# Reloading the weights of a post-norm transformer layer from bf16 copies in DRAM, issued by SyncE

## The reference

```
q = x @ Wq + bq + pe;  k, v = split(x @ Wkv + bkv);  k = k + pe      # 8 heads of 128, one k and v
x = layernorm(x + concat(softmax(causal(q k^T / sqrt(128))) v) @ Wo)
logits = x @ Wc + bc + tie                                            # 128 expert sets, groups of 32 tokens
perm = (logits == max over the 32 tokens of the group)
inner = relu((perm^T x) @ W1 + b1)                                    # per expert set, 1024 -> 32
x = layernorm(x + perm (inner @ W2 + b2))                             # 32 -> 1024, scattered back
```

## Time and profile before

| | |
|---|---|
| median of 3 runs | 5055.51 us (5039.67 to 5063.03) |
| profiled execution, its own time | 5059.08 us |
| its span on the slowest core (core 5) | 5057.5 us |
| spans of the 8 cores | 5020.6 to 5057.5 us |
| mean granted TensorE clock | 0.66 of full speed on every core |

### The profile page before, as it was taken

One profiled execution on the slowest core, in us unless ns is written; L12 is line 12 of the kernel. 1 busy time (PEld: TensorE's weight loads), 2 busy tenths in 40 slices (PEclk: granted clock), 3 DMA queues, 4 the chain that ended last, 5 costly groups with the idle time before them and its releaser, 6 DMA issues.

```text
span 5057.5 us, 64599 instructions; the slowest of 8 cores (5020.6 to 5057.5 us)
## 1 busy us (share of the span) xinstructions
PE 2631.1 (52%) x19792; PEld 1416.4 (28%) x19792; DVE 1497.9 (30%) x3689; ACT 1836.4 (36%) x3808; POOL 54.9 (1%) x104
## 2 busy tenths in 40 slices
PE   4666636332666654542386665463328666546240
PEld 2333314211333322421133332241103333225110
DVE  2322134322322113431332211452223221245132
ACT  0455533210345562321234555241122455523113
POOL 0000000000000000000000000000000000000000
PEclk9678856555777885655577887565557678656555
DMA  4100032465400002157520001216661000200754
GB/s 82 42 17 17 9 50 35 84 124 111 128 17 17 17 9 51 35 105 146 104 92 17 17 17 29 45 20 128 122 133 63 17 18 17 58 18 18 154 100 129
DMA packets 171730, 305.44 MB, mean 60 GB/s; under 512 B 5394, under 2 KB 136722, under 8 KB 166546
## 3 DMA queue, kind: packets, MB, share of 16 engines
q1 hardware_dynamic: 153874, 203.77, 17.3%
q0 software_dynamic: 17536, 97.54, 10.8%
HBM read 298.15 MB, written 100.66 MB: 79 GB/s over the span
## 4 chain that ended last, share of the span: by engine, by line
PE 43%; ACT 17%; DMA 16%; DVE 11%; issue 11%; SPq 1%; ACTq 0%; DVEq 0%; POOL 0%; POOLq 0%
DMA rp_scratch<-rpn 11%; PE pp_pv L368 8%; ACT pT L344 7%; PE pp_s L336 6%; PE pp_w L443 5%; PE pp_s L282 5%; DMA rpe<-rp_scratch 5%; PE pp_s L599 4%; PE pp_s L648 3%; PE pp_s L568 2%; ACT x2b L557 2%; ACT pTn L390 2%; DVE pT L352 2%; PE pp_w L694 2%; PE pp_w L701 2%
## 5 line engine op out<-in xcount | busy, mean ns | idle before, releaser
L344 ACT ACTIVATE pT<-pp_s,c_negC 128x512 bf16<-128x512 f32 x1280 | 846.1, 691 | 354.5 <-PE pp_pv L368 216.9
L368 PE MATMUL pp_pv<-vS,pT 128*128 128x129 bf16 x5120 | 618.6, 257 | 399.0 <-DVE pT L352 230.3
L368 PEld LDWEIGHTS pp_pv<-vS,pT 128*128 128x128 bf16 x5120 | 393.5, 112 | 795.4 <-issue 789.5
L336 PE MATMUL pp_s<-qT,kT 128*128 128x512 bf16 x1280 | 595.3, 483 | 0.1
L352 DVE TENSOR_TENSOR pT<-pT,c_zl 128x512 bf16<-128x512 bf16 x512 | 217.6, 425 | 960.5 <-ACT pT L344 960.3
L648 PE MATMUL pp_s<-w_2t,inr 32*64 32x256 bf16 x1024 | 139.1, 401 | 670.2 <-DVE rpn L661 586.2
L661 ACT CAST rpn<-pp_s 128x256 bf16<-128x256 f32 x256 | 95.4, 373 | 799.0 <-DMA rpe<-rp_scratch 710.4
L282 PE MATMUL pp_s<-xT,w_q 128*128 128x512 bf16 x1024 | 258.2, 422 | 186.8 <-DMA w_kv<-wkv 161.4
L443 PE MATMUL pp_w<-w_o,atT 128*128 128x512 bf16 x1024 | 273.0, 427 | 94.1 <-DVE x L451 80.1
L661 DVE CAST rpn<-pp_s 128x256 bf16<-128x256 f32 x256 | 108.7, 424 | 699.2 <-DMA rpe<-rp_scratch 616.9
L648 PEld LDWEIGHTS pp_s<-w_2t,inr 32*64 32x64 bf16 x1024 | 70.9, 122 | 737.9 <-issue 737.7
(11 more groups left out here) (87 smaller groups left out, 2984.7 us busy)
## 6 DMA issues: line engine op xcount, KB each, us to landing
rp_scratch<-rpn SPq DMA_DIRECT2D x32, 2048.0 KB, 16.0
rpe<-rp_scratch SPq DMA_DIRECT2D x32, 2048.0 KB, 14.4
xtile<-x SPq DMA_DIRECT2D x64, 512.0 KB, 3.8
w<-w POOLq DMA_DIRECT2D x16, 2048.0 KB, 15.4
w_2t<-w2t POOLq DMA_DIRECT2D x64, 512.0 KB, 13.9
y<-x SPq DMA_DIRECT2D x64, 512.0 KB, 4.4
xT<-xT POOLq DMA_DIRECT2D x4, 4096.0 KB, 27.8
w_o<-wo POOLq DMA_DIRECT2D x4, 2048.0 KB, 15.9
```

What stands on the lines that cost most here:

```text
L336: return inc("tensor", "sPE", 1, lambda e, kc=kc, ping=ping, h=h, qb=qb: e.matmul(pp_s[ping][:, :], kT[:, kc * 128: kc * 128 + 128], qT[:, ...
L344: ev = inc("scalar", "sACT", 1, lambda e, ping=ping: e.activation(out=pT[ping][:, :], in_=pp_s[ping][:, :], func=AF.Exp, bias=c_negC, scal ...
L368: ping=ping, sub=sub, kc=kc, kcmax=kcmax: e.matmul(bank[:, colo: colo + 129], pT[ping][:, sub * 128: sub * 128 + 128], vS[:, kc * 132: kc ...
```

## The change

In sequence 0 the weights are loaded by GpSimd as before. When each has landed, SyncE stores the bf16 tile to an internal DRAM tensor (`cwkv`, `cwo`, `ctie`, `cw1`, `cw2`). In sequences 1 to 3 the weights are loaded from these copies by SyncE, without a conversion. `xT` and the weights that stay in SBUF are loaded as before. The waits of each load move from GpSimd's list to SyncE's. Further waits keep reuse of the places in order: in sequence 0 GpSimd waits for the copy of a `w_1` or `w_2t` tile before it loads the next over it, and VectorE and ScalarE wait for the copies before they write over the same places.

```
--- before.py
+++ after.py
+    cw1 = nc.dram_tensor("cw1", [4, 128, 2 * 128 * 32], BF16, kind="Internal").ap()
+    cw2 = nc.dram_tensor("cw2", [4, 128, 32 * 256], BF16, kind="Internal").ap()
+    cwo = nc.dram_tensor("cwo", [128, CH * 1024], BF16, kind="Internal").ap()
+    cwkv = nc.dram_tensor("cwkv", [128, CH * 256], BF16, kind="Internal").ap()
+    ctie = nc.dram_tensor("ctie", [1, T], BF16, kind="Internal").ap()
...
-        mk_wkv = inc("gpsimd", "sGW", 16, lambda e: e.dma_start(out=w_kv, in_=dwkv))
-
+        if s == 0:
+            mk_wkv = inc("gpsimd", "sGW", 16, lambda e: e.dma_start(out=w_kv, in_=dwkv))
+            wait("sync", mk_wkv)
+            st_wkv = inc("sync", "sS3", 16, lambda e: e.dma_start(out=cwkv, in_=w_kv))
+        else:
+            wait("sync", st_all_ws)
+            wait("sync", st_wkv)
+            mk_wkv = inc("sync", "sWE", 16, lambda e: e.dma_start(out=w_kv, in_=cwkv))
+
+        if s == 1:
+            wait("vector", st_s2_all); wait("scalar", st_s2_all)
         wait("tensor", mk_wkv)
+        if s > 0:
+            wait("tensor", mk_xT)
...
         p1_done = now("sPE")
-        wait("gpsimd", p1_done)
-        mk_wo = inc("gpsimd", "sGW", 16, lambda e: e.dma_start(out=w_o, in_=dwo))
-        mk_tie = inc("gpsimd", "sGW", 16, lambda e: e.dma_start(out=c_tie, in_=dtie))
+        if s == 0:
+            wait("gpsimd", p1_done)
+            mk_wo = inc("gpsimd", "sGW", 16, lambda e: e.dma_start(out=w_o, in_=dwo))
+            mk_tie0 = inc("gpsimd", "sGW", 16, lambda e: e.dma_start(out=c_tie, in_=dtie))
+            wait("sync", mk_tie0)
+            inc("sync", "sWS", 16, lambda e: e.dma_start(out=cwo, in_=w_o))
+            st_tie = inc("sync", "sWS", 16, lambda e: e.dma_start(out=ctie, in_=c_tie))
+            mk_tie = mk_tie0
+        else:
+            wait("sync", p1_done)
+            mk_wo = inc("sync", "sWE", 16, lambda e: e.dma_start(out=w_o, in_=cwo))
+            mk_tie = inc("sync", "sWE", 16, lambda e: e.dma_start(out=c_tie, in_=ctie))
...
+                    if s == 0:
+                        wait("sync", st_wkv)
...
-        gw1 = {0: inc("gpsimd", W1S[0], 16, lambda e: e.dma_start(out=w_1[0], in_=dw1[0]))}
+        def w1_load(q4):
+            if s == 0:
+                if q4 >= 2:
+                    wait("gpsimd", w1_store[q4 - 2])
+                m = inc("gpsimd", w1sems[0][q4 % 2], 16,
+                        lambda e, q=q4: e.dma_start(out=w_1[q % 2], in_=dw1[q]))
+                wait("sync", m)
+                w1_store[q4] = inc("sync", ["sS1a", "sS1b"][q4 % 2], 16,
+                                   lambda e, q=q4: e.dma_start(out=cw1[q], in_=w_1[q % 2]))
+                return m
+            return inc("sync", w1sems[1][q4 % 2], 16,
+                       lambda e, q=q4: e.dma_start(out=w_1[q % 2], in_=cw1[q]))
...
+        if s > 0:
+            wait("sync", ln1)
+        gw1 = {0: w1_load(0)}
         def w2t_load(q4, part):
             c0 = 0 if part == 0 else 2048
+            if s == 0:
+                sem = "sW20" if part == 0 else "sW21"
...
+                wait("sync", m)
+                inc("sync", "sS2", 16, lambda e, q4=q4, c0=c0: e.dma_start(
+                    out=cw2[q4][:, c0: c0 + 2048], in_=w_2t[0][:, c0: c0 + 2048]))
+                w2t_store[q4] = inc("sync", "sS2", 16, lambda e, q4=q4, c0=c0: e.dma_start(
+                    out=cw2[q4][:, 4096 + c0: 4096 + c0 + 2048],
+                    in_=w_2t[0][:, 4096 + c0: 4096 + c0 + 2048]))
+                return m
+            sem = "sWC" if part == 0 else "sWD"
+            inc("sync", sem, 16, lambda e, q4=q4, c0=c0: e.dma_start(
+                out=w_2t[0][:, c0: c0 + 2048], in_=cw2[q4][:, c0: c0 + 2048]))
+            return inc("sync", sem, 16, lambda e, q4=q4, c0=c0: e.dma_start(
                 out=w_2t[0][:, 4096 + c0: 4096 + c0 + 2048],
-                in_=dw2[q4][:, 4096 + c0: 4096 + c0 + 2048]))
+                in_=cw2[q4][:, 4096 + c0: 4096 + c0 + 2048]))
...
             if q4 + 1 < 4:
                 if q4 >= 1:
-                    wait("gpsimd", now("sPE"))
+                    wait("gpsimd" if s == 0 else "sync", now("sPE"))
+                gw1[q4 + 1] = w1_load(q4 + 1)
...
             if q4 + 1 < 4:
-                wait("gpsimd", now("sPE"))
+                eng_w = "gpsimd" if s == 0 else "sync"
+                wait(eng_w, now("sPE"))
+                if s == 0:
+                    wait("gpsimd", w2t_store[q4])
                 gw2[q4 + 1] = w2t_load(q4 + 1, 0)
                 gw2b[q4 + 1] = w2t_load(q4 + 1, 1)
```

More of the change, by code:

```diff
@@ L137, in build_nc @@
     semnames = ["sPE", "sACT", "sDVE", "sLD", "sST", "sRS", "sGW",
-                "sXT0", "sXT1", "sW10", "sW11", "sW20", "sW21"]
+                "sXT0", "sXT1", "sW10", "sW11", "sW20", "sW21",
+                "sWA", "sWB", "sWC", "sWD", "sWE", "sWS", "sS1a", "sS1b", "sS2", "sS3"]
     sems, cms = {}, []
@@ L204, in build_nc @@
     prev_stores = None
+    st_all_ws = None
+    st_wkv = None
+    st_s2_all = None; st_s1a = None; st_s1b = None
     def emit_ln_stats_finish():
@@ L470, in build_nc @@
         wait("gpsimd", ln1)
-        gw1 = {0: inc("gpsimd", W1S[0], 16, lambda e: e.dma_start(out=w_1[0], in_=dw1[0]))}
+        w1sems = [["sW10", "sW11"], ["sWA", "sWB"]]
+        w1_store = {}
+        def w1_load(q4):
[10 more added lines that the diff above has]
+                       lambda e, q=q4: e.dma_start(out=w_1[q % 2], in_=cw1[q]))
@@ L472, in w2t_load @@
+        if s == 1:
+            wait("sync", st_all_ws)
+            wait("sync", st_s2_all)
+            wait("sync", st_s1a); wait("sync", st_s1b)
+        if s > 0:
+            wait("sync", ln1)
+        gw1 = {0: w1_load(0)}
         def w2t_load(q4, part):
             c0 = 0 if part == 0 else 2048
-            sem = "sW20" if part == 0 else "sW21"
-            inc("gpsimd", sem, 16, lambda e, q4=q4, c0=c0: e.dma_start(
-                out=w_2t[0][:, c0: c0 + 2048], in_=dw2[q4][:, c0: c0 + 2048]))
@@ L477, in w2t_load @@
-            return inc("gpsimd", sem, 16, lambda e, q4=q4, c0=c0: e.dma_start(
+            if s == 0:
+                sem = "sW20" if part == 0 else "sW21"
+                inc("gpsimd", sem, 16, lambda e, q4=q4, c0=c0: e.dma_start(
+                    out=w_2t[0][:, c0: c0 + 2048], in_=dw2[q4][:, c0: c0 + 2048]))
+                m = inc("gpsimd", sem, 16, lambda e, q4=q4, c0=c0: e.dma_start(
+                    out=w_2t[0][:, 4096 + c0: 4096 + c0 + 2048],
+                    in_=dw2[q4][:, 4096 + c0: 4096 + c0 + 2048]))
+                wait("sync", m)
[5 more added lines that the diff above has]
+                return m
@@ L478, in w2t_load @@
+            sem = "sWC" if part == 0 else "sWD"
+            inc("sync", sem, 16, lambda e, q4=q4, c0=c0: e.dma_start(
+                out=w_2t[0][:, c0: c0 + 2048], in_=cw2[q4][:, c0: c0 + 2048]))
+            return inc("sync", sem, 16, lambda e, q4=q4, c0=c0: e.dma_start(
                 out=w_2t[0][:, 4096 + c0: 4096 + c0 + 2048],
[L479 removed]
+                in_=cw2[q4][:, 4096 + c0: 4096 + c0 + 2048]))
+        w2t_store = {}
         gw2 = {0: w2t_load(0, 0)}
@@ L483, in build_nc @@
         wait("tensor", mk_tie)
+        if s == 0:
+            wait("vector", st_tie)
+            wait("scalar", st_wkv)
         for tb in range(NQB):
@@ L546, in build_nc @@
                 if q4 >= 1:
-                    wait("gpsimd", now("sPE"))
-                gw1[q4 + 1] = inc("gpsimd", W1S[(q4 + 1) % 2], 16,
-                                  lambda e, q=q4 + 1: e.dma_start(out=w_1[q % 2], in_=dw1[q]))
+                    wait("gpsimd" if s == 0 else "sync", now("sPE"))
+                gw1[q4 + 1] = w1_load(q4 + 1)
             if q4 == 0:
@@ L555, in build_nc @@
                     wait("scalar", pv2)
+                    if s == 0:
+                        wait("vector", st_tie); wait("scalar", st_tie)
                 gwait("scalar", ("x2b", tt % 2))
@@ L635, in emit_e2 @@
                 wait("tensor", relu_done)
+                if s == 0:
+                    for eng_ in ("vector", "scalar"):
+                        wait(eng_, w1_store[2]); wait(eng_, w1_store[3])
             rsq_marks = []
@@ L732, in build_nc @@
                 st_m[:, tt: tt + 1], x2[:, tt * 1024: tt * 1024 + 1024], AX.X, ALU.add))
+        if s == 0:
+            wait("scalar", w2t_store[3])
         _ = emit_ln2_finish()
@@ L744, in build_nc @@
         prev_stores = st_marks[-1]
+        if s == 0:
+            st_all_ws = now("sWS")
+            st_s2_all = now("sS2")
+            st_s1a = now("sS1a"); st_s1b = now("sS1b")
         gset("R2xT", sc_last)
```

## The result

The changed kernel takes 5151.78 us (median of 8 runs, 5144.5 to 5170.35) against 5056.82 us (median of 8): a ratio of 1.0195, 95% interval 1.0177 to 1.0213. It is slower by 95 us; the forecast was 5153 us.

A forecast was written before the change was run, and what follows sets the result against it. The kernel was taken as bound by waits, no engine busy over 52%. Terms +88.4 - 6.3 + 15.4 = +97.5 on the profiled 5059.1 gave 5156.6, less 3.6 to the median: 5153 us, range 5110 to 5190.

The forecast's parts named there:

- The seam: Between sequences: w_kv's load waits behind the 16 stores of y, delaying projections by +29.7, +29.9 and +28.8 us, +88.4 in all.
- the drain: Between sequences: w_kv waits some 5 us for store traffic on SyncE's queue; on a second queue the sum would be about 76.
- The clock rival: Delayed projections of sequences 2 and 3 run at a higher TensorE clock, giving 5132 us; chance 0.12.
- The restack of sequences 1 to 3: Second expert layer: first restack behind four faster w_2t loads on SyncE's queue, -2.1 us each, -6.3 in all.
- Sequence 0: Second expert layer, where copies are made: restacks wait for w_2t loads to land, +7.4 and twice +4.0, +15.4 us.
- Restack begins at +18.4: Sequence 0's second expert layer: restack starts 18.4 us after the quarter, following w_2t's landing, second-half copy and issue.
- The covered loads: w_o, w_1 and the first w_2t are issued long before use, so changing their loads costs or gives nothing.
- The slow queue: Second expert layer: slow loads ahead of first restacks and copies fully ahead in sequence 0, giving 5204 us; chance 0.09.
- no stall: Between sequences: w_kv's load passes the stores, so no change, 5065 us; chance 0.04.
- the clock in attention: Longer idle time between sequences lifts the clock in three attention stages, ending faster, 5026 us at 0.95; chance 0.03.

The follow-up runs named there:

- the load moved back: Changed kernel with the w_kv load for the next sequence issued by SyncE ahead of the 16 stores of y: 5065.02 us, ratio 1.0040.
- the part alone: Kernel before with only w_kv copied in sequence 0 and reloaded by SyncE behind the stores of y: 5132.38 us, ratio 1.0169.
- half the stores: Changed kernel with the w_kv load placed behind 8 of the 16 stores of y: ratio 1.0154.
- the changed kernel with two waits: Changed kernel with SyncE's 64 waits ahead of each restack's first store replaced by the last two: 5102.95 us, ratio 1.0122.
- the kernel before with two waits: Kernel before with only the 64 waits ahead of each restack's first store replaced by the last two: 5012.28 us, ratio 0.9923.
- the best kernel: Changed kernel with w_kv ahead of stores, w_2t copies behind the restack, two waits for 64, half the next w_2t early: 4999.4 us, ratio 0.9889.

## Why the prediction was right

- **The seam** (+88.4 forecast, +84.1 measured). Mechanism, place and size hold. It is shown from three sides: the load moved back takes the cost away, the part alone gives it, and half the stores give part of it. The 4 us too many are small only because the pace stands on both sides. I carried sequences 2 and 3 of the profiled core on at 0.27 us a matmul (68.0 and 69.4 us), and in the profile after all three took 57.4 to 57.6 us for 256, or 0.22; but the stages that I subtracted were that core's own, 9 and 11 us longer than the median core's, and the two nearly cancel. The landing was 0.7 to 0.8 us later than forecast in each seam (70.5, 70.2 and 69.4 us after `xT`'s issue, against 69.7, 69.5 and 68.6). The reason given for the drain, that the load shares SyncE's queue, is not borne out: on GpSimd's queue it landed no earlier, and the sum of the seams did not fall to 76.
- **The clock rival** has a grain of truth, not a cause. The slow pace of the earlier trace rows was on 2 of 8 cores of the kernel before (projection stages of 124 to 127 us in sequences 2 and 3), on none after, on none with `w_kv` early or with the seam alone, on two cores of the changed kernel with two waits (147 to 153 us against 144), and on two cores each of the kernel before with two waits (128 to 129 us in sequence 3) and of the best kernel (123 to 126 in sequences 2 and 3). It comes and goes without regard to the seam. In the profile after, the three delayed Q projections ran at a granted clock of 0.96; in that of before it was 0.95 in sequence 1 and 0.81 and 0.79 in sequences 2 and 3. It is in the slowest core's time all the same: the sum gave 5156.6 us for the profiled execution, and the profiled execution after took 5136.4. That the median of eight runs came out at the forecast is in this part luck.
- **The restack of sequences 1 to 3** (-6.3 forecast, -5.7 measured). The sum was right and its working only half so. I let the store queue behind 5.2 us of transfers at 400 GB/s. In fact SyncE was late itself, by the issue of four loads and 64 waits, and the transfers were slower than I took them (windows of the profile after; last the clock, DMA share and GB/s):

```profile
2241.00:2243.00 2.00, 0.73 (x8) 0.37 (x6) 0.81 (x3) 0.81 (x3) 0.00 (x0) 0.50 0.15 18
2243.00:2245.00 2.00, 0.00 (x0) 0.00 (x0) 0.00 (x0) 0.00 (x0) 0.00 (x0) 0.50 0.95 201
2245.00:2247.00 2.00, 0.00 (x0) 0.00 (x0) 0.00 (x0) 0.00 (x0) 0.00 (x0) 0.50 0.90 209
```

  When the store went out at 2247.1, 0.9 of the 2.1 MB had moved; the rest went beside it, and it still landed in 12.4 us against 11.9 alone. With the waits gone the transfers hold the store. Two costs lie side by side there, and either alone gives about the same. The measured term hangs on which profile of the kernel before is taken: with the first restacks of the run with the seam alone it would be -11.7 and not -5.7, and why those differ is open.
- **Sequence 0** (+15.4 forecast, +22.1 measured). This is the mis-sized term. "Restack begins at +18.4" was 20.9, 20.4 and 20.4 us over the cores. I had 15.5 us of landing, 2.6 of the copy's transfer and 0.3 of issue. Measured over the cores, the second copy is issued at 16.5, 15.9 and 16.4 us, and the store 3.3 to 3.7 us behind the end of that issue. The copy's transfer is not in the start, as the store does not wait for it, and it lands in 12.0 us as if alone (11.9). What is there in its place are the 64 waits, which I had at nothing: in restack 0 of the kernel before they had passed one by one while the evictions ran, and after they stand behind the copies. With two waits the starts were 17.4, 17.2 and 17.3. The lower bound of this term, +3.5 with no copy felt, was added up wrongly: 15.5 us of landing give 4.5 + 1.1 + 1.1, or +6.7.
- **The covered loads.** `w_o`, `w_1` and the first `w_2t` cost and gave nothing that shows: attention differs by 0.2, 1.5, -0.5 and 0.4 us, and no weight load is named as a wait of those stages. That half the weight bytes are worth nothing outside the restack fits that; routing and the first expert layer, 1.8 to 3.3 us shorter in three sequences, are within what cores differ by.
- **The slow queue, no stall, and the clock in attention** fell with the table: first restacks of 38 us, seams of 144, attention unchanged.

The errors of -4.3, +6.7 and +0.6 and the -5.1 of the other stages nearly cancel; the median was met within 2 us, more closely than the terms deserve.

## What to carry to other kernels

A load that is moved to another engine takes that engine's place in line as well as its speed: read what stands ahead of it in the new program and what each of those waits for, before counting bytes. A faster transfer that nobody waited for is worth nothing, and 0.5 MB issued 62 us late cost 84 us in three seams, where the faster loads gave 6. A list of waits that were met long ago is not free: when one late wait stands ahead of them, they are worked off one after the other on the path, and the last of each semaphore is enough.

## What was not expected of the hardware

- A wait on SyncE that is already met costs 0.05 us. 64 of them took 3.3 us in the chain, and taking 62 away in every restack gave 10 us a sequence in the kernel before.
- A load on the software queue beside stores on SyncE's queue did not land earlier than one behind them on the same queue: 8.1, 8.6 and 7.5 us against 8.4, 8.3 and 7.5, in one profile each, and the stage was 144.2 us in both.
- Four software loads of 0.5 MB issued together with a store of 2 MB on SyncE's queue hardly touched it (12.9 us against 11.9 alone), and made the next one, issued 13.8 us after them, 27.5 us long instead of 19.3.
- The stores ahead, 16 of them at 1.09 us each, and `w_kv` behind them kept the DMA engines of the changed kernel full until 1355, over 7 us after the last issue. Windows (busy us per engine; last the clock, DMA share, GB/s):

```profile
1340.00:1345.00 5.00, 0.00 (x0) 0.00 (x0) 0.00 (x0) 5.00 (x6) 0.00 (x0) 0.50 1.02 352
1353.00:1355.00 2.00, 0.00 (x0) 0.00 (x0) 0.00 (x0) 0.00 (x0) 0.00 (x0) 0.50 1.02 420
1355.00:1357.00 2.00, 0.48 (x2) 0.23 (x3) 0.00 (x0) 0.00 (x0) 0.00 (x0) 0.50 0.13 51
```

SyncE issued 16 stores of 0.5 MB in 17.5 us, which is 480 GB/s. While it did, the engines, at their full share, moved 350 to 360 GB/s (420 only after the last issue), so the backlog is what is issued faster than it is moved.
